# Probabilities times values: two products in place of three, with the halves added on GpSimd

## What is computed

```
q, k, v = split(x @ w_qkv.T + b_qkv)          # 32 query heads, 8 key/value heads, 32 wide
q, k = apply_rope(q), apply_rope(k)
scores = where(causal, q @ k^T / sqrt(32), -1e20)
attn = softmax(scores)
out = attn @ v                                # each value head serves 4 query heads
```

## Time and profile before

| What | us |
|---|---|
| median of 3 runs | 1196.9 |
| lowest and highest of them | 1192.68, 1198.27 |
| the profiled execution's own time | 1195.03 |
| its span, first to last instruction | 1193.2 |
| PE busy in it | 1159.9 |
| DVE busy | 720.0 |
| ACT busy | 422.0 |
| POOL busy | 208.4 |

### The profile page before, as it was taken

How to read it: one execution, slowest core, us unless ns; L and a number is a source line. 1 busy time by engine, 2 the same in 40 slices (tenths; PEclk the granted TensorE clock), 3 DMA queues, 4 the chain that set the end, 5 groups by cost and what they waited for, 6 DMA issues and landing times.

```text
span 1193.2 us, 18765 instructions
## 1 busy us (share of the span) xinstructions
PE 1159.9 (97%) x6920; PEld 1040.4 (87%) x6920; DVE 720.0 (60%) x1222; ACT 422.0 (35%) x1196; POOL 208.4 (17%) x133
## 2 busy tenths in 40 slices
PE   8999999999999999999989999999999899999998
PEld 8999988888888888888879998888887688888886
DVE  5312128878788888888874227444445866666664
ACT  5212124455545555555454223212123422222221
POOL 0000114433343344444350002000000000000000
PEclk9999999999999999999999999999999899999999
DMA  6111032111111111110323114555544322222212
GB/s 251 37 37 53 9 100 80 45 45 61 44 45 51 44 44 44 44 53 26 102 80 107 55 71 169 184 173 180 178 175 159 124 107 106 106 102 85 80 71 89
DMA packets 42151, 107.79 MB, mean 90 GB/s; under 512 B 5106, under 2 KB 16242, under 8 KB 42098
## 3 DMA queue, kind: packets, MB, share of 16 engines
q1 hardware_dynamic: 42098, 107.07, 25.6%
HBM read 73.50 MB, written 33.55 MB: 90 GB/s over the span
## 4 chain that ended last, share of the span: by engine, by line
PE 91%; DVE 5%; ACT 1%; DMA 1%; issue 1%; POOL 1%; SPq 0%; DVEq 0%; ACTq 0%; POOLq 0%
PE psum L1024 22%; PE psum L1643 13%; PE psum L389 13%; PE psum L1976 13%; PE psum L1396 8%; PE psum L2037 4%; PE psum L1086 4%; PE psum L1956 4%; PE psum L1056 3%; PE psum L1071 2%; PE psum L1043 1%; PE psum L1103 1%; PE psum L1659 1%; DVE low L894 1%; DVE rows L1563 1%
## 5 line engine op out<-in xcount | busy, mean ns | idle before, releaser
L1024 PE MATMUL psum<-p_h,c_high_low 128*128 128x512 f32 (+1 forms) x768 | 196.4, 359 | 0.5 <-DVE qkv L980 0.5
L1024 PEld LDWEIGHTS psum<-p_h,c_high_low 128*128 128x128 f32 x768 | 133.5, 188 | 13.3 <-issue 0.7
L389 PE MATMUL psum<-c_high_low,w_h 128*128 128x256 f32 x768 | 135.3, 286 | 5.0 <-ACT w_h L499 4.9
L389 PEld LDWEIGHTS psum<-c_high_low,w_h 128*128 128x128 f32 x768 | 117.2, 195 | 5.2 <-issue 5.2
L1396 PE MATMUL psum<-chunk,rows 128*128 128x384 f32 (+1 forms) x576 | 107.3, 342 | 4.8 <-DVE rows L1266 2.4
L1396 PEld LDWEIGHTS psum<-chunk,rows 128*128 128x128 f32 x576 | 102.6, 190 | 5.5 <-issue 5.4
L1024 PE MATMUL psum<-p_l,c_high_low 128*128 128x512 f32 (+1 forms) x384 | 104.3, 366 | 0.0
L389 PE MATMUL psum<-c_high_low,w_l 128*128 128x256 f32 x384 | 100.3, 286 | 0.0
L1643 PE MATMUL psum<-rows,ring 128*128 128x512 f32 x384 | 93.0, 397 | 0.0
L1643 PE MATMUL psum<-rows,at 128*128 128x512 f32 x384 | 90.4, 391 | 0.0
L1643 PEld LDWEIGHTS psum<-rows,ring 128*128 128x128 f32 x384 | 71.3, 188 | 17.2 <-DVE ring L1588 0.5
(11 more groups left out here) (182 smaller groups left out, 2308.5 us busy)
## 6 DMA issues: line engine op xcount, KB each, us to landing
ring_plain<-in_x_t SPq DMA_DIRECT2D x32, 256.0 KB, 2.6
attn_scratch<-ring_plain SPq DMA_DIRECT2D x16, 512.0 KB, 2.7
scratch_plain<-attn_scratch SPq DMA_DIRECT2D x16, 512.0 KB, 5.4
x_tok<-in_x_tok SPq DMA_DIRECT2D x16, 512.0 KB, 4.3
x_scratch<-x_out SPq DMA_DIRECT2D x16, 512.0 KB, 5.9
x_t_scratch<-x_t SPq DMA_DIRECT2D x16, 512.0 KB, 2.7
raw<-x_t_scratch SPq DMA_DIRECT2D x16, 512.0 KB, 4.1
rest<-x_scratch SPq DMA_DIRECT2D x16, 512.0 KB, 4.1
```

The costliest lines, as they stand in the source:

```text
L389: mm = pe.matmul(to, stationary, moving, start=start and n == 0, stop=k == KT - 1 and n == len(passes) - 1, skip_group_check=True)
L1024: mm = pe.matmul(to, sx[:, k, :], moving(w, n, k), start=first, stop=False, skip_group_check=True)
```

## The change

The stationary block of a product now holds the high and the low values of two heads side by side (`vb`: 2 x 2 x 32 = 128 columns). One product with `pt_h` gives high by high on partitions 0 to 63 and low by high on partitions 64 to 127. A second product with `pt_l` uses only the first 64 columns of the block and adds high by low onto partitions 0 to 63. `attend(b)` makes 4 products of each kind, 8 in place of 12.

What comes with it: each b now fills both banks (4 and 5), so `attend(b = 1)` waits until b = 0 has been copied out; DVE copies partitions 0 to 63 to `attn` and ACT copies partitions 64 to 127 to a new tile `beside`, two instructions each for every b; POOL adds the two; the store waits for POOL. POOL clears one tile at the start of the stage in place of two. Two semaphores (`f1_w0_high`, `index_in`) are merged with others of the first stage; the waits stay where they were.

```diff
-    vb_h, vb_l = (sb(n, [P, BPU, QUADS, 2, 4, HD], F32R) for n in ("vb_h", "vb_l"))
+    vb = sb("vb", [P, BPU, QUADS, 2, 2, 2, HD], F32R)
+    beside = sb("beside", [P, KT, BPU, SEQ])
...
+    def values(part, j):
+
+        return s_ps[part * SEQ:(part + 1) * SEQ, :, j * GRP * SEQ:(j + 1) * GRP * SEQ].rearrange("p q (g t) -> p q g t", g=GRP)
+
+    def by_head(t, b, j):
+        return t[j * SEQ:(j + 1) * SEQ, :, b, :].rearrange("p (q g) t -> p q g t", q=QUADS)
...
# ACT
             act.wait_ge(pv_done, 2 * w + b + 1)
             if b == 0:
-                need(act, stored, 16 * w)
-            act.activation(attn[:, :, b, :], s_ps[:, b, :].rearrange("p (k t) -> p k t", k=KT), ACT.Copy).then_inc(pv_out, 1)
+                need(act, pv_sum, 2 * w)
+            for j in range(2):
+                last = act.activation(by_head(beside, b, j), values(1, j), ACT.Copy)
+            last.then_inc(pv_low, 1)
...
# POOL
+        def values_sum(w, b):
+            pool.wait_ge(pv_low, 2 * w + b + 1)
+            pool.wait_ge(pv_high, 2 * w + b + 1)
+            pool.tensor_tensor(attn[:, :, b, :], attn[:, :, b, :], beside[:, :, b, :], ALU.add).then_inc(pv_sum, 1)
...
+            if value:
+                values_sum(w, 0)
+                values_sum(w, 1)
             if nxt:
                 split_x(u + 1, 0)
...
# DVE
+        def values_out(w, b):
+            dve.wait_ge(pv_done, 2 * w + b + 1)
+            if b == 0:
+                need(dve, stored, 16 * w)
+            for j in range(2):
+                last = dve.tensor_copy(by_head(attn, b, j), values(0, j))
+            last.then_inc(pv_high, 1)
...
             if value:
+                values_out(w, 0)
                 probs_low(w, 1)
             if score and not main:
                 fold2.low_row(dve, 2, after_other=True)
                 fold2.low_row(dve, 3)
+            if value:
+                values_out(w, 1)
             if score:
                 dve.wait_ge(qk_high, 3 * v + 1)
...
# PE, scores and attend
-                need(pe, pv_out, 2 * v)
+                need(pe, pv_low, 2 * v)
+                need(pe, pv_high, 2 * v)
...
-            n = 0
-            for vv, pp in ((vb_h, pt_h), (vb_l, pt_h), (vb_h, pt_l)):
+            else:
+                pe.wait_ge(pv_low, 2 * v + 1)
+                pe.wait_ge(pv_high, 2 * v + 1)
+            for parts, pp in ((2, pt_h), (1, pt_l)):
                 if pp is pt_l:
                     pe.wait_ge(pt_low, 2 * v + b + 1)
                 for q in range(QUADS):
                     for j in range(2):
-                        mm = pe.matmul(s_ps[:, b, q * 4 * SEQ:(q + 1) * 4 * SEQ], vv[:, b, q, j, :, :].rearrange("p c d -> p (c d)"),
-                                       pp[:, q, j, :, :].rearrange("p g t -> p (g t)"), start=n == 0, stop=pp is pt_l and j == 1, skip_group_check=True)
-                        n += 1
+                        v_at = vb[:, b, q, j, 0:parts, :, :].rearrange("p m h d -> p (m h d)")
+                        mm = pe.matmul(s_ps[0:parts * SEQ, q, j * GRP * SEQ:(j + 1) * GRP * SEQ], v_at, pp[:, q, j, :, :].rearrange("p g t -> p (g t)"),
+                                       start=parts == 2 and j == 0, stop=parts == 1 and j == 1, skip_group_check=True)
...
# POOL, once
-        pool.memset(vb_h[:, :, :, :, :, :].bitcast(F32), 0.0).then_inc(vb_zero, 1)
-        pool.memset(vb_l[:, :, :, :, :, :].bitcast(F32), 0.0).then_inc(vb_zero, 1)
+        pool.memset(vb[:, :, :, :, :, :, :].bitcast(F32), 0.0).then_inc(vb_zero, 1)
```

More of the change, by code:

```diff
@@ L473, in folding_qkv @@
     lead_in, lead_high, lead_low = sem("f1_lead_in"), sem("f1_lead_high"), sem("f1_lead_low")
-    w0_in, w0_high = sem("f1_w0_in"), sem("f1_w0_high")
+    w0_in = sem("f1_w0_in")
     raw, high, low = fold.raw_chunk(0), fold.c_h[:, fold.buffer(0), 0:HALF, :], fold.c_l[:, fold.buffer(0), 0:HALF, :]
@@ L498, in scalar @@
         act.wait_ge(w0_in, 16)
-        act.activation(fold.w_h[:, 0, left], fold.w_raw[0][:, left], ACT.Copy).then_inc(w0_high, 1)
+        act.activation(fold.w_h[:, 0, left], fold.w_raw[0][:, left], ACT.Copy).then_inc(lead_high, 1)
         act.wait_ge(fold.w_loaded[0], 16)
@@ L531, in lead @@
     def lead(pe):
-        pe.wait_ge(lead_high, 1)
-        pe.wait_ge(w0_high, 1)
+        pe.wait_ge(lead_high, 2)
         for n in range(3):
@@ L600, in attention @@
     low_ps = t_ps[:, 1, 0:P]
-    const_in, index_in = sem("const_in"), sem("index_in")
+    const_in, index_in = sem("const_in"), sem("f1_lead_in")
     x_in = [sem("x_in0"), sem("x_in1")]
@@ L613, in attention @@
     v_high, v_low, vb_zero, vb_high, vb_low = (sem(n) for n in ("v_high", "v_low", "vb_zero", "vb_high", "vb_low"))
+    pv_high, pv_low, pv_sum = (sem(n) for n in ("pv_high", "pv_low", "pv_sum"))
     s_done, s_masked, s_max, s_sub, s_exp, s_sum, s_inv, s_norm = (
@@ L616, in attention @@
     pt_done, pt_high, pt_low = sem("pt_done"), sem("pt_high"), sem("pt_low")
-    pv_done, pv_out, stored = sem("pv_done"), sem("pv_out"), sem("attn_stored")
+    pv_done, stored = sem("pv_done"), sem("attn_stored")
     consts = [(b_bc[:, :], a["b_qkv"].partition_broadcast(P)), (cos[:, :], a["cos"]), (sin[:, :], a["sin"]),
@@ L626, in q_ps, with diag @@
         return t_ps[:, turn, at * P:(at + n) * P].rearrange("p (n b t) -> p n b t", n=n, b=BPU)
-    def diag(vb, b, h):
-        flat = vb[h * SEQ:(h + 1) * SEQ, b, :, :, :, :].rearrange("p q j c d -> p q (j c d)")
-        return flat.rearrange("p q (m d) -> p q m d", d=HD)[:, :, h:h + 7:6, :]
+    def diag(part, b, h):
+        return vb[h * SEQ:(h + 1) * SEQ, b, :, :, part, h, :]
+    def values(part, j):
+        return s_ps[part * SEQ:(part + 1) * SEQ, :, j * GRP * SEQ:(j + 1) * GRP * SEQ].rearrange("p q (g t) -> p q g t", g=GRP)
+    def by_head(t, b, j):
+        return t[j * SEQ:(j + 1) * SEQ, :, b, :].rearrange("p (q g) t -> p q g t", q=QUADS)
     TURNS = [(0, ["k0", "k1", 0, 1]), (1, [2, 3, 4, 5]), (0, [6, 7])]
@@ L679, in step @@
             if value:
-                sp.wait_ge(pv_out, 2 * w + 2)
+                sp.wait_ge(pv_sum, 2 * w + 2)
                 sp.dma_start(a["attn"][bass.ds(w, 1), :, :].rearrange("o p c -> (o p) c"),
@@ L688, in sync @@
         sp.dma_start(index[:, :], a["labeler"]).then_inc(index_in, 16)
-        sp.wait_ge(index_in, 16)
+        sp.wait_ge(index_in, 16 * 2)
         load_a(0)
@@ L771, in step @@
                 act.wait_ge(v_high, v + 1)
-                act.wait_ge(vb_zero, 2)
+                act.wait_ge(vb_zero, 1)
                 need(act, pv_done, 2 * v)
@@ L775, in step @@
                     for h in range(2):
-                        last = act.activation(diag(vb_h, b, h), v_hl[b * SEQ:(b + 1) * SEQ, 0, :, :, h, :].bitcast(F32), ACT.Copy)
+                        last = act.activation(diag(0, b, h), v_hl[b * SEQ:(b + 1) * SEQ, 0, :, :, h, :].bitcast(F32), ACT.Copy)
                 last.then_inc(vb_high, 1)
@@ L819, in normalise @@
                                ALU.mult).then_inc(s_norm, 1)
+        def values_sum(w, b):
+            pool.wait_ge(pv_low, 2 * w + b + 1)
+            pool.wait_ge(pv_high, 2 * w + b + 1)
+            pool.tensor_tensor(attn[:, :, b, :], attn[:, :, b, :], beside[:, :, b, :], ALU.add).then_inc(pv_sum, 1)
         def step(u, main, score, value, nxt):
-            v = u - 1
+            v, w = u - 1, u - 2
             if score and not main:
@@ L935, in step @@
                 dve.wait_ge(v_low, v + 1)
-                dve.wait_ge(vb_zero, 2)
+                dve.wait_ge(vb_zero, 1)
                 need(dve, pv_done, 2 * v)
@@ L939, in step @@
                     for h in range(2):
-                        last = dve.tensor_copy(diag(vb_l, b, h), v_hl[b * SEQ:(b + 1) * SEQ, 1, :, :, h, :].bitcast(F32))
+                        last = dve.tensor_copy(diag(1, b, h), v_hl[b * SEQ:(b + 1) * SEQ, 1, :, :, h, :].bitcast(F32))
                 last.then_inc(vb_low, 1)
@@ L1485, in tensor @@
     def tensor(pe):
-        pe.wait_ge(fold.sem("pv_out"), 2 * UNITS)
+        pe.wait_ge(fold.sem("pv_low"), 2 * UNITS)
+        pe.wait_ge(fold.sem("pv_high"), 2 * UNITS)
         pe.wait_ge(fold.lb_low, 1)
```

## The result

The changed kernel takes 1239.67 us in the median of 4 runs (1236.1 to 1240.22), the kernel before 1197.59 us beside it (1192.68 to 1199.24): ratio 1.0352, interval 1.0316 to 1.0389. It is slower, as forecast, but by 42 us and not by 27, and outside of the range of 1210 to 1234. The other three took 1239.24 to 1240.22 us, at a mean granted clock of 0.974 or 0.975 where the profiled one has 0.978.

What follows compares the result with a forecast made beforehand. DVE, not the 97% busy PE, was taken to bound the second `attend`. 14 units x (1.4 + 0.5) us, plus 2.1, less 0.5, gave 28.2 us more: 1224 us, range 1210 to 1234 (the forecast's own range 1216 to 1233).

Steps and rivals of the forecast that it cites:

- DVE's two copies: Copies of b = 0 queue on DVE ahead of `pt_l` of b = 1, 0.69 us each: 1.4 us a unit.
- The reading: At the second `attend` PE already waits some 0.1 us for DVE, which has no room between rotation and `pt_l`.
- The products: Eight fewer PE products a unit, 0.118 us each, narrow ones too: the 0.94 us gain is all spent in waits.
- The low end: DVE's copies of b = 0 read faster, saving 0.27 us each: 0.84 us for both; called less likely.
- ACT's further copy of b = 1: A second ACT copy ahead of `keys` delays the low queries 0.60 us and so the scores: 0.5 us a unit.
- The sum: 14 units x (1.4 + 0.5) = 26.6 us, plus 2.1 for step 16, less 0.5 for step 17: 28.2 us.
- step 16: Both pairs of DVE's copies stand ahead of the low queries, so the scores start later: 2.1 us taken.
- step 17: First `attend` waits for its parts either way; the second has its data and gains four products: -0.5 us.
- PE as the bound: Rival: PE decides and the removed products are simply gone, 15 us faster, 1182 us; chance 0.06.
- cheap copies: Rival: copies cost 0.84 us on DVE, 0.4 through ACT, 18.2 us in all, 1214 to 1215; chance 0.12.
- Width changes: Rival: changing block width drains PE, 0.33 us more a unit, 1230 us; chance 0.14, shared with POOL's second addition.
- POOL's second addition holding DVE's low keys: Rival: POOL's addition after the copies of b = 1 delays DVE's low keys up to 0.3 us; chance 0.14, shared with width changes.

Runs made afterwards that it cites:

- drop8: Kernel before without the four products of low values by high probabilities in each `attend` (8 of 24 a unit): 1196.77 us, ratio 1.0006.
- old_vlow: Kernel before with the low part of the values (0.34 us on DVE) moved behind `pt_l` of b = 1: 1193.9 us, ratio 0.9982.
- old_dve: Kernel before with the copy of b = 0 made on DVE ahead of `pt_l` of b = 1, in two instructions, not on ACT: 1217.48 us, ratio 1.0164.
- act_b0: Changed kernel with all four copies of b = 0 on ACT, so none on DVE ahead of `pt_l` of b = 1: 1206.3 us, ratio 1.0066.
- spread_pool: `spread` with POOL's second addition of a unit moved behind the low part of x: 1206.53 us, ratio 1.0085.
- warm: Changed kernel with 12 more thrown-away PE products in each step 2 to 15, where PE waits for DVE's copies of b = 0: 1226.09 us, ratio 1.0237.
- wide: Changed kernel with 128 columns in the stationary block of the `pt_l` products too, so none is narrow: 1239.08 us, ratio 1.0334.
- spread: `act_b0` with ACT's high-part copies of b = 0 behind `pt_h` of b = 1 and one copy of b = 1 between high keys: 1214.04 us, ratio 1.0153.

## Why the prediction was right and where it was wrong

**The step that failed** is in the paragraph on DVE's two copies: PE waits until 321.6, makes four products, waits until 322.82, "makes four and goes on at 323.3", and from there the unit goes on as before. The two waits were priced at their length, and what they do to PE's clock was put at nothing without a reason. In 10 of 14 units the clock was at its lower level behind them, for 3.7 us at 0.54 in the one shown, which cost some 0.95 us in each. The path that the forecast named, through DVE's queue, was right.

**The reading was right.** "At the second `attend` DVE is already the one that PE waits for, by a hair": drop8 shows it from one side, old_vlow from the other. And DVE was late there because of the rotation product beside POOL's instruction, as the forecast says; only, that product did not end with POOL's instruction (319.12) but at 319.80.

**The products.** 0.118 us each was right, for the narrow ones too, and that none of the 0.94 us of a unit reaches the end was right (drop8, and the unit at full clock).

**DVE's two copies.** Forecast 1.4 us a unit, measured 1.36 in the changed kernel and 1.44 as the longer unit of old_dve. The low end (0.84) did not happen: the pair took 1.37. In act_b0, without them ahead of `pt_l`, a unit takes 28.2 us, 1.4 less than the 29.6 of a unit at full clock.

**ACT's further copy of b = 1.** Forecast 0.5, measured 0.53 and another 0.1 within the first product, in units at full clock. In the ten units that lost the clock this wait is not seen: PE reached the scores late itself. That ACT is behind the wait is read from the rows (DVE's low queries wait for ACT's high ones). No run takes the copy away; spread_pool, which moves it behind two high keys, still waits 0.32 us at the scores.

**The sum lacks one term: PE's clock.** The forecast took 0.118 us and full speed for every product behind the waits. In steps 2 to 15 the span grew by 37.4 us (4 units by 2.0, 10 by 2.95; forecast 26.6). With the clock held it would have been 14 x 2.0 = 28. The other 9.4 are the clock, some 0.95 in each of ten units; warm, which holds it, has no unit above 29.6. At 1226.09 us warm lies within the range and 2 us from the forecast of 1224. In a unit that lost the clock PE takes 6.34 us from the transposes to the scores (333.66 to 340.00) in place of 5.26; so the slow stretch first eats the wait for the low queries and then costs another microsecond.

The rest of the 41.1 us: the start of the stage is 0.5 later, step 16 cost 2.4 (forecast 2.1), and step 17 with all that follows cost 0.8 where 0.5 of gain was forecast. There the clock is down behind PE's waits too, 0.73 in this window:

```profile
669.53:680.00 10.47, 10.47 (x50) 10.47 (x51) 3.92 (x6) 2.21 (x3) 2.56 (x2) 0.73 0.01 3
```

In step 16 it is down as well (PE's two rows of four products at 632.18 and 633.03 have 1.06 and 1.05 us for the usual 0.63). What these three small parts consist of was not tested by itself.

**The rivals.** PE as the bound, cheap copies: did not happen. Width changes: excluded by wide. POOL's second addition holding DVE's low keys: not in the changed kernel, where it ran from 335.38 to 336.66 and the low keys ran from 336.87 on, 1.67 us for four (1.66 before); but it was 0.2 us away, and it is what spread lost by.

**The range** was too narrow because a unit's two new waits were priced at their length alone. The waits are in the forecast ("idle time before the first `attend` products of b = 1 put down to DVE's copy, a second before the `pt_l` products"); what a gap of PE does to the work behind it is not.

What stays open: why four of the fourteen units kept the clock. They are steps 2, 3, 9 and 10. All fourteen have the same two waits, 1.52 or 1.53 us and 0.45 or 0.46, so their length alone does not say whether a unit loses the clock.

## What to carry to other kernels

A busy share of 97% does not make an engine the bound at each place. Look at the waits that are nearly nothing, because behind each of them another engine may be just as late: here a wait of 0.1 us. Work added on that engine ahead of it cost its full length (old_dve, 1.4 us a unit), and work taken from the busy engine gave nothing (drop8). Before DVE gets a new instruction, ask which instruction comes behind it in the queue and who waits for that one. And price a new wait of PE at more than its length: where the clock fell behind it here, PE ran almost wholly at half clock for 3.7 us, and filling the gap with products that nobody needs paid (warm).

## What was not expected of the hardware

- PE's granted clock fell in 10 of 14 units behind waits of 1.53 and 0.46 us with four products between, though PE was busy for 93% of such a unit (28.36 of 30.57 us). In the units shown it did not fall behind one wait of 1.27 us (old_dve), 0.79 us (drop8) or 0.67 us (act_b0), nor behind 0.46 us alone (warm). The Trainium skill, page TensorE: Matmul & The Clock Gate, Part 1: The HAM clock gate, says that PE gets half its clock when it has been idle; the two levels agree, but in this unit PE was never idle for longer than 1.53 us and lost the clock all the same.
- 168 products that nobody needs made the kernel 14 us faster in the median, 10 between the profiled executions (warm).
- A block of 64 columns loads faster than one of 128, 134 for 188 ns in the median of the weight loads below (lowest, median and highest ns, then first and last start), but the products stay 0.118 us apart:

```profile
L1117 PEld LDWEIGHTS psum<-pt_h,vb x128: 186/188/335, 205.0 to 675.4; 128*128 128x128 f32 x128
...
L1117 PEld LDWEIGHTS psum<-pt_l,vb x128: 132/134/232, 205.5 to 675.9; 128*64 128x64 f32 x128
```

The Trainium skill, page TensorEngine Tiling (Array Packing), Key Properties, says that PE runs empty at a change of tiling mode. No such cost shows here; whether a block of 64 columns is such a change at all, no run here tells.
